# Maxima of both score tiles of a double bank in one VectorE instruction over 1024 columns

## The reference

```
h = h + attention(layernorm(h))      # 8 heads, keys and values shared by the heads
h = h + experts(layernorm(h))        # 6 experts, the best 2 weighted
...
scores = einsum('bhsd,bdt->bhst', q, k) * scale
attn = softmax(scores, axis=-1)      # over 512 keys
ctx = einsum('bhst,btd->bhsd', attn, v)
```

## Time and profile before

| | us |
|---|---|
| median of 3 runs | 801.54 |
| lowest and highest run | 798.57, 805.35 |
| the profiled execution | 804.77 |
| its span, from the first to the last instruction | 802.9 |
| mean granted clock of TensorE, share of full speed | 0.97 |

### The profile page before, as it was taken

How to read it: one execution, slowest core, us unless ns; L and a number is a source line. 1 busy time by engine, 2 the same in 40 slices (tenths; PEclk the granted TensorE clock), 3 DMA queues, 4 the chain that set the end, 5 groups by cost and what they waited for, 6 DMA issues and landing times.

```text
span 802.9 us, 31729 instructions
## 1 busy us (share of the span) xinstructions
PE 702.3 (87%) x14160; PEld 390.1 (49%) x14160; DVE 568.3 (71%) x1079; ACT 476.1 (59%) x1200; POOL 299.2 (37%) x366
## 2 busy tenths in 40 slices
PE   5688879898998999898998999898998999999871
PEld 4445436454554446444554446444554445554631
DVE  6477755867867786867767786867768687677537
ACT  2456575686557765586467765576566756676220
POOL 1143111621665127521565117531566118310804
PEclk8799999999999999999999999999999999999996
DMA  4000000000000000000000000000000000000000
GB/s 155 1 2 2 2 2 2 3 3 2 4 16 3 3 2 17 2 2 2 4 17 2 3 2 16 3 2 3 3 16 3 2 3 11 8 3 2 2 15 14
DMA packets 9448, 7.22 MB, mean 9 GB/s; under 512 B 8672, under 2 KB 8800, under 8 KB 9184
## 3 DMA queue, kind: packets, MB, share of 16 engines
q1 hardware_dynamic: 9312, 5.20, 2.1%
HBM read 3.10 MB, written 2.10 MB: 6 GB/s over the span
## 4 chain that ended last, share of the span: by engine, by line
PE 64%; DVE 22%; ACT 6%; issue 4%; POOL 3%; DMA 0%; SPq 0%; DVEq 0%; ACTq 0%; POOLq 0%
PE m_bank L415 25%; PE s_bank L389 21%; DVE nmax L720 8%; ACT p L617 4%; PE f_bank L482 4%; DVE e2t L889 3%; PE s_bank L401 2%; PE s_bank L528 2%; DVE st L735 2%; POOL st L982 1%; PE s_bank L544 1%; PE s_bank L517 1%; DVE st L743 1%; PE s_bank L452 1%; PE f_bank L498 1%
## 5 line engine op out<-in xcount | busy, mean ns | idle before, releaser
L617 ACT ACTIVATE p<-s_bank,nmax 128x512 f32<-128x512 f32 x512 | 347.5, 687 | 237.3 <-DVE nmax L720 236.6
L720 DVE TENSOR_REDUCE nmax<-s_bank 128x1 f32<-128x512 f32 x512 | 327.3, 682 | 111.7 <-PE s_bank L389 110.9
L389 PE MATMUL s_bank<-kf,g 64*64 64x512 f32 x2048 | 267.1, 607 | 37.4 <-ACT p L617 29.5
L415 PEld LDWEIGHTS m_bank<-p,woz 128*32 128x32 f32 x8192 | 222.5, 112 | 113.5 <-issue 113.0
L415 PE MATMUL m_bank<-p,woz 128*32 128x128 f32 x8192 | 256.4, 278 | 10.8 <-POOL woz L963 10.8
L963 POOL TENSOR_TENSOR woz<-cst,rz 128x256 f32<-128x256 f32 x128 | 81.0, 654 | 339.0 <-DVE rz L725 339.0
L389 PEld LDWEIGHTS s_bank<-kf,g 64*64 64x64 f32 x2048 | 63.8, 133 | 146.1 <-ACT p L617 84.2
L617 ACT ACTIVATION_READ_ACCUMULATOR p<-s_bank,nmax 128x1 f32 x512 | 102.9, 201 | 0.0
L730 DVE STREAM_TRANSPOSE m<-m_bank 128x512 f32<-128x512 f32 x64 | 45.7, 713 | 32.0 <-PE m_bank L415 31.1
L982 POOL TENSOR_TENSOR st<-st,power 128x8 f32<-128x8 f32 x24 | 39.9, 1664 | 56.8 <-DVE st L745 56.3
L266 POOL TENSOR_TENSOR y<-y,gt 128x768 f32<-128x768 f32 x30 | 44.3, 1476 | 36.0 <-DVE y L903 36.0
(11 more groups left out here) (110 smaller groups left out, 498.0 us busy)
## 6 DMA issues: line engine op xcount, KB each, us to landing
tower_out<-o SPq DMA_DIRECT2D x16, 128.0 KB, 2.4
cst<-consts SPq DMA_DIRECT2D x1, 1166.0 KB, 8.7
m<-ids SPq DMA_DIRECT2D x1, 896.0 KB, 6.0
cst<-consts SPq DMA_DIRECT2D x1, 544.0 KB, 4.3
cst<-consts SPq DMA_DIRECT2D x1, 288.0 KB, 6.3
m<-ids SPq DMA_DIRECT2D x1, 128.0 KB, 2.4
cst<-consts SPq DMA_DIRECT2D x1, 3.5 KB, 2.2
```

Of the source, the lines that this page charges most:

```text
L389: last = pe.matmul(double[half(q), 512 * r:512 * r + 512], g[half(r), a // 2 % 2, a % 2, first:first + 64], kf[half(r), par, a // 4, :], s ...
L415: last = pe.matmul(m_bank[quarter(r), 128 * n:128 * n + 128], woz[:, a % 2, 2 * mm + hh, 32 * oh:32 * oh + 32], keys[:, r, :, :], start=(m ...
L617: nc.scalar.activation(p[:, c % 16, :], bank("S", i, c - r)[:, 512 * r:512 * r + 512], ACT.Exp, bias=nmax[:, c % 16:c % 16 + 1], accum_out ...
L720: nc.vector.tensor_reduce(nmax[:, c % 16:c % 16 + 1], bank("S", i, c - r)[:, 512 * r:512 * r + 512], AX.X, ALU.max, negate=True).then_inc( ...
```

## The change

DVE's `maxima` takes both tiles of a double bank in one instruction: 128 by 2 by 512 in, two columns of `nmax` out. It waits for the scores of both tiles, and raises `maxed` by two. It is called in even slots only, so all other work of an even slot, which stood between the two maxima, stands behind both.

```diff
             def maxima(i, c):
-                r = c % 2
-                dve.wait_ge(score, SLOTS * i + c + 1)
-                nc.vector.tensor_reduce(nmax[:, c % 16:c % 16 + 1], bank("S", i, c - r)[:, 512 * r:512 * r + 512],
-                                        AX.X, ALU.max, negate=True).then_inc(maxed, 1)
+
+                dve.wait_ge(score, SLOTS * i + c + 2)
+                nc.vector.tensor_reduce(nmax[:, c % 16:c % 16 + 2], bank("S", i, c)[:, :].rearrange("q (r t) -> q r t", r=2),
+                                        AX.X, ALU.max, negate=True).then_inc(maxed, 2)
...
                 for slot in range(SLOTS):
-                    maxima(i, slot)
+                    if slot % 2 == 0:
+                        maxima(i, slot)
```

## The result

The changed kernel takes 817.62 us (median of 4 runs, 816.61 to 818.59); the kernel before, in the same comparison, 800.48 us (798.57 to 805.35). The ratio is 1.0205, with a 95% interval of 1.0156 to 1.0254. The profiled execution took 817.23 us, with a span of 815.4.

What follows compares the result with a forecast made beforehand. PE sets the pace, DVE matters where the chain leaves PE and comes back. Six middle iterations 18.4, iteration 0 -2, last +1.7: +18 on 801.54 gives 820 us, range 806 to 834.

Steps and rivals of the forecast that it cites:

- The wait for the second tile: At each pair's maxima: both tiles' scores end together, so waiting for both costs 0, bounds 0 and 0.5 us.
- The walk through a middle iteration: PE's lateness followed slot by slot through slots 0 to 63: +3.07 us in each of six iterations, 18.4 us.
- Iteration 0: First iteration, with Fourier steps between maxima: new order shortens PE's waits, about -2 us, bounds -5 and +2.
- The last iteration: No prep and no next query there: -0.3 + 0.52 + 0.54 + 0.98 = +1.7 us.
- One sign that I had named for being wrong: A granted clock below 1.00 past iteration 0 would show the prediction wrong.
- The gain at slot 32: In iteration 0, a Fourier step of 2.09 us no longer stands between the two maxima: a gain of 1.4 us.
- A second tile 0.2 us later: Part of the costly rival: the second tile's scores end 0.2 us after the first's, as much again, 834 us.
- One or two losses of 8 us to the clock: Part of the costly rival: PE's longer waits lower its clock, 8 us per iteration hit, giving 835 to 845 us.
- The slack at slot 28: Exp 25 and PE's pair stand 0.82 us apart: no slack, so later exponentials make PE late there, D = +0.36.
- the faster case: Rival at slots 12 to 25: the new order wins if PE's slack behind slot 25 were 1 us; 795 us, chance 0.06.
- The case of no change: Rival: only existing waits grow, slots 28, 36 and 55 don't become new ones; +4, 806 us, chance 0.14.
- The costly case: Rival: wide maximum takes 1.36 us, 827; second tile later, 834; or PE's clock falls, 835 to 845; chance 0.17.

Runs made afterwards that it cites:

- e8: The changed kernel with two narrow maxima in the even slot instead of the wide one, both waiting for the scores of both tiles; 796.03 us.
- e1: The changed kernel with two narrow maxima of 512 columns in each even slot instead of the wide one, other work behind both; 795.17 us.
- e6: As e1, with PE's transposes of x moved from slot 23 to slot 24, behind that slot's score pair; 795.57 us.
- e7: As e1, but with the wide maximum at the 11 pairs of slots 0, 22, 24, 32, 34, 40, 42, 48, 54, 56 and 62; 819.22 us.
- e11: The kernel before, unchanged, run once more for a second trace; 800.06 us.
- e2: As e1, but ACT takes neither exponential of a pair before both maxima are done; 826.46 us.
- e3: The changed kernel with narrow maxima at 11 pairs, where the walk has the first exponential ending a wait, and wide ones at the other 21; 799.05 us.
- e5: The changed kernel with six matmuls on zeros, 1.5 us, ahead of PE's wait for POOL's x at slot 23; 818.55 us.
- e9: As e1, with six matmuls on zeros, 1.5 us, ahead of PE's wait for POOL's x at slot 23; 793.42 us.
- e4: The changed kernel with the wide maximum at the end of the even slot, behind that slot's other work; 835.15 us.

## Why the prediction was right

**The price of the instruction** was forecast at 1.21 us and is 1.219. The latency from the start of the maxima to PE, 1.24 + 1.50, is exact. The wait for the second tile, taken as nothing, is 0.06 us, with 0.07 more for the wide instruction (e8).

**The walk through a middle iteration** holds at its end, and less well in its middle. How late PE is against the iteration before, in us, forecast and as the trace has it in an iteration at full clock (start 307.40) and in one that lost it (start 401.11):

| place | forecast | full clock | clock lost |
|---|---|---|---|
| slot 23, transposes of x | -0.71 | -0.77 | -0.76 |
| slot 25, behind xt | -0.22 | -0.82 | +0.20 |
| slot 28 | +0.36 | -0.28 | +0.32 |
| slot 36 | +0.88 | +0.38 | +0.93 |
| slot 43, query | +1.40 | +1.04 | +1.59 |
| slot 52 | +1.90 | +1.52 | +2.07 |
| slot 59, query | +2.88 | +2.46 | +3.01 |
| next iteration | +3.07 | +2.82 | +3.38 |

At full clock the steps from slot 28 on are near the sizes that I gave them: 0.5 to 0.7 us at slots 28, 36, 43 and 52, 0.94 at 59; at 63 it is 0.36, where I had 0.19. Two things were missed, and it is luck that they cancel.

First, xt comes 0.8 us earlier in that iteration, where the forecast had 0.22. The rstd at slot 21 takes 0.17 us, and 1.06 before. It runs beside POOL's scaling of x, and its length goes with which of the two starts first: in the changed kernel DVE starts 0.05 us ahead of POOL, in the kernel before 0.01 behind it. In one middle iteration before it took 0.17 as well, and that one is 0.5 us shorter (90.41). The order of the change does not by itself bring this: e1, e6 and e7 have it, and rstd starts 0.01 behind and takes 1.06 in all six. e7, without this gain, takes 94.08 us at full clock, +3.2 for a forecast of 3.07.

Second, the walk did not follow what the wait for x becomes: 2.03 us, since PE is 1.74 us earlier there and x only 0.77. Behind it the clock falls in three of six iterations, which are then 0.5 to 0.9 us longer than the other three. The mean over six is +3.0: (683.19 - 119.79) / 6 = 93.90 us, against 90.85 before. Forecast 18.4 us for the six, measured 18.3.

**Iteration 0** is the term that was mis-sized: -2 us forecast, with bounds of -5 and +2; measured, from H1 to H1, -7.6 against the first trace and -3.9 against e11. Up to the first H1 the changed kernel is 0.8 and 1.1 us slower, where I had a gain of 0.3. The order shortens PE's waits there as forecast, and keeps the clock up as well, which the sum left out. **The last iteration**: +1.7 forecast, +2.7 measured (85.84 against 83.18 us from its start to the products behind it).

**The sum against the time.** Against the first trace the span grew by only 12.5 us, because that execution had a slow iteration 0 and 1.7 us of low clock at the end. Against e11 it grew by 17.2: +1.1 up to the first H1, -3.9 in iteration 0, +17.3 in the middle ones, +2.7 in the last, nothing behind it. That is near the difference of the medians (17.1), for a forecast of 18. So the total is this near in part by luck: errors of 1 to 2 us in each of the terms, of both signs, offset each other.

**The signs.** A middle iteration of 93.9 us with PE busy for 84.0, the new waits at slots 28 and 36, 1.64 us at slot 59 and none at slot 22 are as forecast. The waits for exponentials reach 6.2 us, not 7, and the longest wait of a reciprocal is at slot 23 (1.38 us), not at 55 (0.60). One sign that I had named for being wrong did appear: a clock below 1.00 past iteration 0, in three of six middle iterations. The mechanism of the loss stands on e1, e2 and e7 even so.

**Slips in the sums.** The gain at slot 32 adds up to 1.3 us, not 1.4. A second tile 0.2 us later costs 7 x 0.2 x 7 = 10 us, not 7, so 837 and not 834. One or two losses of 8 us to the clock give 828 or 836 from 820, so one of them lies inside the range. None of this touches the forecast of 820.

**The rivals.** The slack at slot 28 was as small as the two rows said; with it the faster case was out. In part its place was right: e1 shows the new order to be worth 0.5 us in a middle iteration at full clock. The case of no change fell with e3 and e7: the waits at slots 28 and 36 are there. The costly case had one true part: a longer wait of PE did cost clock, 0.5 to 0.9 us and not 8 in an iteration. The sentence of the Trainium skill (Perfetto Trace Analysis, Optimizing Scalar/DVE Operations) on breaking up instructions of an engine that isn't saturated is borne out by e1 against the changed kernel, by 22 us. Its 125 ns of overhead for an instruction on PSUM, as what merging would save, is not: the maxima's busy time fell by 17.7 us, 69 ns for each instruction saved.

## What to carry to other kernels

When two results feed a consumer one by one, merging the producer's instructions delays the first result by nearly a whole instruction; count the places where that first result ends a wait on the path (here at most 11 of 32), multiply for an upper bound (11 x 0.53 = 5.8 us in an iteration; e7 against e1 at full clock shows 3.7, or seven times 0.53), and compare with the engine time saved only if that engine is the bound. Judge a merge and the reordering that comes with it apart: here the one cost 22 us and the other gained 7. A gain ahead of a fixed wait makes that wait longer, and here TensorE's clock fell behind such waits in some iterations. Filling the wait kept the clock up in the traces, but the filler costs its own time (1.4 us) where there is no wait to fill.

## What was not expected of the hardware

- TensorE's clock after a wait of 2.0 us was at times 1.00 and at times lower (0.72 over six microseconds around the end of the wait), in iterations of the same program with the same waits. After its waits of 1.64 us at slot 59 the clock was 1.00 in all six middle iterations.
- With six matmuls in that wait, so that 0.5 us of it is left, the clock was 1.00 in all middle iterations of e5 and e9.
- A wait of 2 us was not needed: the clock fell behind waits of 1.2 and 1.3 us, 2.4 us apart, in all six middle iterations of e4, and behind 0.27, 0.63 and 1.25 us in one of six of e6.
- The tensor_scalar over 8 columns on DVE (rstd) beside POOL's scaling of x (1.04 us) took 1.06 us where it started 0.01 us behind POOL (before, e1, e6, e7) and 0.17 where it started 0.05 us ahead of it (the changed kernel).
- A wait for both tiles of a pair ends only 0.06 us after a wait for the first (e8 against e1), though the pair takes 1.09 us.
